# Attention weights loaded, rounded and split in column halves, with a reordered tail

## The reference

```
x = layernorm(x + attention(x))          # Wq, Wkv, Wo: 16 heads of 64, then + bo
x = layernorm(x + mlstm(x, ctx, ctx))    # 4 heads of 64, gates from x and ctx
x = layernorm(x + ffn(x))                # 8 experts 256 -> 1024 -> 256, top 2 of a softmax
# ffn(x) = x + sum over the two chosen experts of
#          score * (expert(xn) - c_expert + c_total),  c_e = relu(b1_e) @ W2_e + b2_e
```

## Time and profile before

| | us |
|---|---|
| median of 3 runs (773.53 to 775.21) | 774.41 |
| the profiled execution | 772.59 |
| its span | 770.8 |
| TensorE busy | 701.1 (91%) |
| VectorE busy | 471.3 (61%) |
| ScalarE busy | 333.5 (43%) |
| GpSimd busy | 269.1 (35%) |

### The profile page before, as it was taken

How to read it: one execution, slowest core, us unless ns; L and a number is a source line. 1 busy time by engine, 2 the same in 40 slices (tenths; PEclk the granted TensorE clock), 3 DMA queues, 4 the chain that set the end, 5 groups by cost and what they waited for, 6 DMA issues and landing times.

```text
span 770.8 us, 15170 instructions
## 1 busy us (share of the span) xinstructions
PE 701.1 (91%) x5128; PEld 609.8 (79%) x5129; DVE 471.3 (61%) x1085; ACT 333.5 (43%) x992; POOL 269.1 (35%) x227
## 2 busy tenths in 40 slices
PE   4699999999999999998989989999999999999860
PEld 4689787888989798886869978888888888788640
DVE  4243536586877778587778855555555555555465
ACT  4566666676766667767423112212222222122202
POOL 2300000120604223050644555177067200478973
PEclk9999999999999999999777999999999999999955
DMA  8358485651011010100513244155134311112233
GB/s 305 101 168 293 146 269 173 220 175 43 29 29 56 15 50 22 44 28 16 191 55 110 68 159 151 48 160 175 41 118 157 119 35 40 64 40 83 76 100 119
DMA packets 67681, 82.68 MB, mean 107 GB/s; under 512 B 5884, under 2 KB 59688, under 8 KB 67624
## 3 DMA queue, kind: packets, MB, share of 16 engines
q1 hardware_dynamic: 58984, 52.54, 21.3%
q0 software_dynamic: 8640, 29.38, 11.8%
HBM read 45.04 MB, written 36.86 MB: 106 GB/s over the span
## 4 chain that ended last, share of the span: by engine, by line
PE 72%; POOL 9%; ACT 7%; DVE 6%; issue 4%; DMA 1%; POOLq 0%; ACTq 0%; SPq 0%; DVEq 0%
PE bank L996 12%; PE bank L748 8%; PE bank L749 7%; PE bank L750 7%; PE bank L868 4%; PE bank L966 4%; PE bank L968 4%; PE bank L967 4%; PE bank L939 4%; PE bank L976 4%; PE bank L905 3%; PE bank L917 3%; ACT arena L1096 3%; POOL arena L717 3%; POOL arena L726 1%
## 5 line engine op out<-in xcount | busy, mean ns | idle before, releaser
L996 PE MATMUL bank<-w_ring,hidT_hi 128*128 x320 | 119.8, 408 | 1.2 <-DVE hidT_lo L1637 1.2
L1214 ACT ACTIVATE hidT_hi<-bank 128x512 fp32r<-128x512 f32 x80 | 43.5, 596 | 172.3 <-PE bank L976 168.1
L1096 ACT ACTIVATE arena<-bank,negmx 128x128 f32<-128x128 f32 x256 | 90.8, 377 | 7.0 <-DVE negmx L1249 7.0
L996 PE MATMUL bank<-w_ring,hidT_lo 128*128 x320 | 83.3, 281 | 0.0
L1610 DVE TENSOR_TENSOR arena<-bank,b_rep 128x512 f32<-128x512 f32 x80 | 55.3, 692 | 40.9 <-PE bank L968 40.5
L1616 DVE TENSOR_REDUCE work<-bank 128x256 f32<-128x512 f32 x40 | 27.7, 691 | 78.0 <-PE bank L996 78.0
L966 PE MATMUL bank<-w_ring,xgT_hi 128*128 x160 | 66.8, 417 | 4.6 <-DVE xgT_lo L1629 2.8
L996 PEld LDWEIGHTS bank<-w_ring,hidT_hi 128*128 128x128 f32 x320 | 60.1, 188 | 12.6 <-issue 1.6
L623 POOL TENSOR_TENSOR rsq<-ssq,neghalf 128x8 f32<-128x8 f32 x8 | 13.2, 1646 | 158.4 <-DVE ssq L1351 158.2
L1255 DVE RECIPROCAL rinv<-rsum 128x8 f32<-128x8 f32 x32 | 6.5, 203 | 94.7 <-ACT arena L1096 89.9
L968 PE MATMUL bank<-w_ring,xgT_lo 128*128 x160 | 63.0, 393 | 0.0
(11 more groups left out here) (252 smaller groups left out, 1901.8 us busy)
## 6 DMA issues: line engine op xcount, KB each, us to landing
xg_dram<-zeros SPq DMA_DIRECT2D x9, 2176.0 KB, 9.4
w_raw<-in_L_ffn_W_dram POOLq DMA_DIRECT2D x16, 1024.0 KB, 6.5
y_dram<-zeros SPq DMA_DIRECT2D x2, 2560.0 KB, 10.6
work<-xg_dram SPq DMA_DIRECT2D x40, 128.0 KB, 2.1
y_dram<-work SPq DMA_DIRECT2D x40, 128.0 KB, 1.7
b_rep<-in_L_ffn_b_dram POOLq DMA_DIRECT2D x8, 512.0 KB
work<-gmax_dram SPq DMA_DIRECT2D x14, 256.0 KB, 3.8
arena<-in_x_dram SPq DMA_DIRECT2D x8, 256.0 KB, 2.7
```

Source lines behind the costliest of these rows:

```text
L996: last = pe.matmul(o, l, r, start=c == 0 and l is both[0], stop=c == FC - 1 and l is both[0])
L1096: last = nc.scalar.activation(probs[:, n % 2, h * S:(h + 1) * S], ps_score[:, h * S:(h + 1) * S], ACT.Exp, bias=negmx[:, n % 2, h:h + 1], ...
```

## The change

Nothing is computed differently but the order of sums in six shares. At the start:

- the three attention weights are loaded in six DMAs of 512 columns, first halves first; ScalarE rounds and VectorE splits them by halves. ScalarE rounds the first halves ahead of the first copy and the second halves ahead of the copy of the first value unit; VectorE splits the second halves behind the first maxima. TensorE waits for the half it reads;
- TensorE runs 4 dummy matmuls before and 8 behind the first transposes;
- TensorE's wait for Wo's split moves to the first output projection;
- VectorE's waits for bo, x, the small parameters and gamma move from ahead of step 1's maxima to the end of step 3 of the first pair.

In the middle, GpSimd doubles the input behind `split(5, 1)` instead of behind the last split. In the tail:

- the lower shares of the first six sequences are one multiply-add each on VectorE, behind the constants' operand; GpSimd's `add_low` is left with ten;
- `rstd_of` stands ahead of gathers 9 and 13 instead of 8 and 12;
- the shift and first row of a quad are computed inside the next quad, behind its second sequence (`normalise_out`), with two sets of small buffers; in the last quad VectorE scales two rows and ScalarE two.

```diff
-            sp.dma_start(wq_raw, wq.rearrange("(c p) n -> p c n", p=P)).then_inc(wq_loaded, 16)
...
+            for half in range(2):
+                n = slice(half * 512, (half + 1) * 512)
+                for k, (raw, w) in enumerate(((wq_raw, wq_v), (wk_raw, wkv_v[:, :, 0:INNER]), (wv_raw, wkv_v[:, :, INNER:]))):
+                    sp.dma_start(raw[:, :, n], w[:, :, n]).then_inc(wqkv_loaded[half][k], 16)
...
+                if e == E - 3:
+                    pool.tensor_tensor(xres[:, :, :], xres[:, :, :], xres[:, :, :], ALU.add).then_inc(input_doubled, 1)
...
             for b in range(B):
-                gather(0, b, low_gathered[b % 4])
-                if b >= 2:
+                gather(0, b, first_gathered if b < BY_DVE else low_gathered[b % 4])
+                if b >= BY_DVE + 2:
                     add_low(b - 2)
...
-                if b % 4 == 0 and b >= 8:
+                if b % 4 == 1 and b >= 8:
                     rstd_of(b // 4 - 2)
...
-                    if p == 0 and g == 0:
-                        pe.wait_ge(attn_split, "qk".index(kind) + 1)
+                    if p == 0 and g % 2 == 0:
+                        pe.wait_ge(attn_split, 3 * (g // 2) + "qk".index(kind) + 1)
...
+            fill(4)
+            run(FIRST[0:1])
+            fill(8)
+            run(FIRST[1:])
             scores(0)
-            pe.wait_ge(wo_split, 1)
...
+            rounds = {("q", 0, 0): [(0, 0), (0, 1), (0, 2)], ("v", 0, 0, 0): [(1, 0), (1, 1), (1, 2)]}
...
+            for part in range(2):
+                n = slice(part * 512, (part + 1) * 512)
+                for k, (hi, lo, raw) in enumerate(attn_w):
+                    dve.wait_ge(attn_rounded, 3 * part + k + 1)
+                    dve.tensor_tensor(lo[:, :, n], raw[:, :, n], hi[:, :, n].bitcast(F32), ALU.subtract)\
+                        .then_inc(attn_split, 1)
+                if part == 0:
+                    maxima(0)
             weights_of(0)
...
+            def normalise_out(q):
+                dve.wait_ge(rstd4_ready, q + 1)
+                k = q % 2
+                dve.scalar_tensor_tensor(shift4[k][:, :], mv4[k][:, :, 0], -1.0, rstd4[k][:, :], ALU.mult, ALU.mult)\
+                    .then_inc(shift_ready, 1)
+                for b in range(1 if q < QUADS - 1 else 2):
+                    last = dve.tensor_scalar(xres[:, 4 * q + b, :], y_all[:, 0, 4 * q + b, :], mv4[k][:, b, 0:1],
+                                             rstd4[k][:, b:b + 1], ALU.subtract, ALU.mult)
+                last.then_inc(out_ready, 1)
+
+            dve.wait_ge(input_doubled, 1)
+            dve.wait_ge(first_gathered, 16 * BY_DVE)
+            for b in range(BY_DVE):
+                last = dve.scalar_tensor_tensor(y_all[:, 0, b, :], y_all[:, 0, b, :], share[:, 0, b:b + 1], xres[:, b, :],
+                                                ALU.mult, ALU.add)
+            chain.link(last)
...
                     if b + 4 < B:
+                        if b + 4 >= BY_DVE:
+                            dve.wait_ge(low_added, b + 5 - BY_DVE)
                         constants_in(b + 4)
+                    if q and b % 4 == 1:
+                        normalise_out(q - 1)
```

More of the change, by code:

```diff
@@ L210, in decoder_layer @@
         stats4 = sb("stats4", [P, 4, 6])
[L211 to L214, removed]
+        mv4 = [sb(f"mv4_{k}", [P, 4, 2]) for k in range(2)]
+        ve4, rstd4, shift4 = ([sb(f"{name}_{k}", [P, 4]) for k in range(2)] for name in ("ve4", "rstd4", "shift4"))
         score = sb("score", [P, 2, B])
@@ L265, in decoder_layer @@
         xs_loaded = sem("xs_loaded")
-        wq_loaded = sem("wq_loaded")
+        wqkv_loaded = [[sem(f"w{kind}{half}_loaded") for kind in "qkv"] for half in range(2)]
         attn_rounded = sem("attn_rounded")
@@ L774, in unit @@
                     b, half = a
-                    if p == 0 and b + half == 0:
-                        pe.wait_ge(attn_split, 3)
+                    if p == 0:
+                        pe.wait_ge(attn_split, 3 * half + 3)
                     t, n = slice(b * S, (b + 1) * S), slice(INNER + half * 512, INNER + (half + 1) * 512)
@@ L873, in out_proj @@
             def out_proj(i, b, half):
+                if i + b + half == 0:
+                    pe.wait_ge(wo_split, 1)
                 pe.wait_ge(oT_split, i * STEPS + 2 * half + b + 1)
@@ L920, in weighted_sums, with fill @@
                 last.then_inc(oT_done, 1)
+            def fill(n):
+                for _ in range(n):
+                    pe.matmul(bank[6][:, 0:P], ident[:, :], ident[:, :], start=True, stop=True)
             pe.wait_ge(ident_ready, 3)
-            run(FIRST)
+            fill(4)
+            run(FIRST[0:1])
+            fill(8)
+            run(FIRST[1:])
             scores(0)
-            pe.wait_ge(wo_split, 1)
             for i in range(PAIRS):
@@ L935, in _ @@
                     weighted_sums(n)
-            def fill(n):
-                for _ in range(n):
-                    pe.matmul(bank[6][:, 0:P], ident[:, :], ident[:, :], start=True, stop=True)
             pauses = {("N", A): 10, ("T", Y): 4, ("L", A): 6, ("R", A): 3, ("U", Z, 0): 22, ("R", Y): 20, ("N", Z): 34,
@@ L1139, in round_early @@
                                .rearrange("p (g n) -> p g n", n=n)).then_inc(w_rounded, 1)
-            rounds = {("q", 0, 0): [(wq_loaded, wq_hi, wq_raw), (wk_loaded, wkv_hi[:, :, 0:INNER], wk_raw)],
-                      ("k", 0, 0): [(wv_loaded, wkv_hi[:, :, INNER:], wv_raw)]}
+            attn_w = ((wq_hi, wq_raw), (wkv_hi[:, :, 0:INNER], wk_raw), (wkv_hi[:, :, INNER:], wv_raw))
+            rounds = {("q", 0, 0): [(0, 0), (0, 1), (0, 2)], ("v", 0, 0, 0): [(1, 0), (1, 1), (1, 2)]}
             for un in FIRST:
-                for loaded, hi, raw in rounds.get(un, []):
-                    act.wait_ge(loaded, 16)
-                    nc.scalar.copy(hi, raw).then_inc(attn_rounded, 1)
+                for part, k in rounds.get(un, []):
+                    n = slice(part * 512, (part + 1) * 512)
+                    act.wait_ge(wqkv_loaded[part][k], 16)
+                    nc.scalar.copy(attn_w[k][0][:, :, n], attn_w[k][1][:, :, n]).then_inc(attn_rounded, 1)
                 copy_unit(un)
@@ L1234, in _ @@
                 act.wait_ge(shift_ready, q + 1)
-                for b in range(1, 4):
+                for b in range(1 if q < QUADS - 1 else 2, 4):
                     last = nc.scalar.activation(xres[:, 4 * q + b, :], y_all[:, 0, 4 * q + b, :], ACT.Identity,
-                                                bias=shift4[:, b:b + 1], scale=rstd4[:, b:b + 1])
-                last.then_inc(out_ready, 1)
+                                                bias=shift4[q % 2][:, b:b + 1], scale=rstd4[q % 2][:, b:b + 1])
+                last.then_inc(out_scaled, 1)
         @block.vector
```

60 lines of the change are left out of this document (28 added, 32 removed).

## The result

Five runs of the changed kernel have a median of 769.36 us (767.91 to 770.43), beside 774.41 us (773.47 to 775.88) for the kernel before in the same comparison: a ratio of 0.9932, 95% interval 0.9915 to 0.9949. It is faster, by 5.1 us, not by the 13.5 us forecast, and outside the range. The profiled span went from 770.8 to 767.7 us; forecast was 757.3.

The account below looks back on a forecast made before the run. TensorE in its own order was taken as the bound between the two ends. Terms 4.5 + 0 + 5.0 + 3.5 + 0.5 = 13.5 us off 774.4 gave 760.9 us, range 757.5 to 765.8.

Parts of the forecast that it names:

- Start, -4.5 us: First 40 us: loading and splitting attention weights by halves starts projections and scores earlier, 4.5 us less.
- The collision: At the start, VectorE's second-half splits and GpSimd's output-weight split block each other, ending at 25.7 us.
- Doubled input, 0: Middle: doubling the input was already hidden behind a wait, so moving it behind expert 5's split gives 0 us.
- A quad normalised inside the next and the last quad, -4.0 us: Tail: three VectorE waits for GpSimd's power go, -3.5 us; last quad's rows shared two and two, -0.5 us.
- The layout: Tail schedule worked out on paper: quads of 5.3, 5.7, 5.7 and 4.5 us, gathers landing 0.4 to 1 us early.
- Six lower shares, -5.0 us: Tail: six shares moved from GpSimd to VectorE let VectorE's first quad start at 734.8 instead of 739.82 us.
- Rival (b): Tail: upper gathers become the bound, slowed beside VectorE's multiply-adds; VectorE waits about 3 us, 764 us; chance 0.13.
- Rival (d): Drain between attention and experts: more time at the lower granted clock makes the kernel slower; chance 0.03.

Follow-up runs that it names:

- experiment 11: The kernel before with only the changed start (weights loaded, rounded and split by halves); 769.50 us, ratio 0.9940.
- Experiment 4: The changed kernel with no lower shares on VectorE: GpSimd adds all sixteen, each with its gather; 766.46 us, ratio 0.9903.
- experiment 7: The changed kernel with gathers interleaved, at most four in a row, and VectorE's six lower multiply-adds ahead of the last tile's rows_out; 762.14 us, ratio 0.9846.
- experiment 9: The changed kernel, nine gathers in a row untouched, plus 35 small wait-free operations each on VectorE and ScalarE around tile 35; 769.58 us in one run.
- experiments 5 and 6: The changed kernel with 126 idle semaphore increments ahead of tile 35, in ScalarE's stream (769.63 us), then in both ScalarE's and VectorE's (768.88 us).
- experiment 3: The changed kernel with VectorE's six lower gathers issued behind GpSimd's ten, which keep their adds between them; 761.98 us, ratio 0.9834.
- experiment 13: The changed kernel with 60 small wait-free copies on ScalarE in the tail, beside upper gathers five to nine; 767.02 us in one run.
- experiment 10: The changed kernel with GpSimd's first lower gather held until tile 36's hidden products are done, so the same nine gathers run later; 768.34 us, ratio 0.9921.

## Why the prediction was wrong

- **Start, -4.5 us: right in its mechanism, with luck in the number.** Alone it gives 5.0 us (experiment 11). First projection at 7.85 us (7.9), third scores at 34.71 (34.1). The collision was where it was expected, and the second halves ended at 26.3 us (25.7): one split of 5.53 us against 1.2 for its like. The Trainium skill ("SBUF — State Buffer", section "Who interferes with whom") was the reading that held. What the sum had at nothing is the landing of the key half: ScalarE waited 1.28 us for it at 7.72, and the first scores came at 16.03, not 15.2. So the trace has 3.9 us, and the 1.2 us of clock that make it 5.1 were in no term. By VectorE's sixth maximum (68.32 before, 64.78 here) the traces of the other kernels with this start lie between 64.35 and 67.37, and those whose key half was split at 10 us or later (here at 8.80) are among the last.
- **Doubled input, 0: right**, shown by the idle of 11.19 us.
- **A quad normalised inside the next and the last quad, -4.0 us: too high by 1.0.** Experiment 4 is the start, the moved doubling and these; beside experiment 11 it has 766.46 - 769.50 = -3.0 us. The layout said that the gathers hold by 0.4 to 1 us. In the trace the quads take 22.6 us (739.29 to 761.9), not 21.2: VectorE waits 0.29 and 0.37 us for the power and 0.75 us for a gathered row, all three at nothing in the layout.
- **Six lower shares, -5.0 us: the step that failed.** The sum took six multiplies and six adds from GpSimd and priced what that does to GpSimd and VectorE. It did not ask what the gathers do to others once nothing paces them, and so had the tiles before the tail at no cost. With the row broken up the term is -4.5 us (766.46 to 761.98); as built it is +2.9 us, since the row costs 769.36 - 761.98 = 7.4 us (7.8 in the trace). -5.0 - 3.0 - 4.5 + 7.4 = -5.1 us is the measured gain by construction, each figure being a difference of two of these medians; it checks nothing.
- **Inside that term, the right number for another reason.** The first upper multiply-add was to come 8.9 us behind the last rows_out (734.8 - 725.91), bound by VectorE. It came 9.1 us behind it (739.29 - 730.21), but VectorE was ready 1.24 us earlier and waited for the second gather, which took 2.48 us.
- **Rival (b)** was right in its mechanism as far as the traces go: the one upper gather issued beside six multiply-adds in a row took 2.48 us, and in experiment 7, which has none there, the same gather takes 0.96. But it is one gather of sixteen, and VectorE's waits for gathers come to 1.24 + 0.75 us instead of 3. Experiment 7 shows that moving the six only moves the collision. It is already inside the -4.5.
- **Rival (d)**, the clock of the drain, took 1.6 us in one trace, through fills that ended 2.2 us behind the rows they covered instead of 0.6.

Not settled: by what the gathers hold the two engines. Shown is that at the tiles it takes indirect gathers, issued 1.25 us apart; that four do not do it and six do; that the hold begins 7.3 us after the first (experiment 9) and ends 1.4 to 3.4 us after the last; that TensorE goes on, and that plain transfers issued at more than twice the rate do nothing. Two things fit no theory of mine: rows_out comes 5.7 us late with two waits and one operation to do, longer than a trickle of 0.71 us explains; and in the tail, beside nine upper gathers in a row, ScalarE's copies trickle, later than 7.3 us, while VectorE does not.

The Trainium skill ("Runtime: NRT & Kernel Launch", section "Instruction fetch mechanics") has each engine fetch its program through a DMA queue of its own, in blocks, mostly hidden. A fetch held up by the gathers would fit the trickle, but the traces speak against it, as experiments 5 and 6 do. The DMA view lists packets of instruction queues by themselves. The changed kernel has none between 691.2 and 716.3 us, and experiment 3, whose engines run freely there, has none from 692.1 to 705 us either, so none seems to have been due. In experiment 13 one of 8 KB lies in the middle of the trickle, at 742.74 us, and took 0.31 us; in experiment 10 one of 16 KB at 706.84 us took 1.15 us. In the kernel before such packets take 0.31 to 0.55 and 0.88 to 1.47 us. Not shown is to which engine a packet belongs, and whether one was asked for late. Not tried either is whether recording the trace, which every run here carries, has a part in the hold.

## What to carry to other kernels

When work is taken out of a queue between transfers, the work was also their pacing: price the transfers' new rate for every other engine, not only the work removed. Here it was enough to keep GpSimd's ten remaining adds between the gathers, and the same six shares went from a loss of about 2.9 us to a gain of 4.5. Judge a part of a change by the kernel with that part alone taken back: the sum of the whole was faster and hid a part that made it slower.

## What was not expected of the hardware

- A row of unpaced indirect gathers held VectorE and ScalarE: nothing at four, 1.5 us of VectorE and nothing of ScalarE at six, 5.3 to 5.7 us at nine (4.6 to 6.4 with experiments 5, 6 and 10), 13.7 us of ScalarE at sixteen (18.00 less its normal 4.27). Paced by adds or by landing it held neither.
- Within it, operations without any wait started in groups on a common step of 0.71 us on both engines (experiment 9, one run).
- After 5 us without work TensorE's next 16 products of a tile's output took 5.48 us instead of 2.82, with a granted clock of 0.59 from 704 to 710 us: about a third of the cost of the stall came after it had ended.
- Six multiply-adds on VectorE took 2.45 us beside one gather, which grew to 2.48 us, and 4.93 us beside GpSimd's adds and a gather.
